# A small projection in the scan stage with two products a tile instead of three, its low-part rows added by VectorE, and C's rows copied apart

## What is computed

```python
xz = x @ W_in.T
x_proj, z = jnp.split(xz, 2, axis=-1)          # 1024 channels each
x_conv = _silu(conv_b + sum(xp[:, k:k + l, :] * conv_w[:, k] for k in range(4)))
x_dbl = x_conv @ W_xproj.T                      # 1024 channels to 33 values
Bmat, Cmat = x_dbl[..., :16], x_dbl[..., 16:32]
dt = jnp.clip(jax.nn.softplus(x_dbl[..., -1]), 0.001, 0.1)
# scan over time: h = exp(dt A) h + dt B x ;  y = h C
y = y * _silu(z) + x_conv * D_param
return y @ W_out.T
```

## Time and profile before

| | |
|---|---|
| runs, median (lowest to highest) | 2617.36 us (2613.93 to 2620.7) |
| the profiled execution: time | 2616.86 us |
| its span, first to last instruction | 2615.2 us |
| TensorE busy with products | 2416.5 us (92%), 16951 of them |
| TensorE loading weights | 2128.4 us (81%) |
| VectorE busy | 1492.4 us (57%) |
| ScalarE busy | 1199.3 us (46%) |
| GpSimd busy | 648.2 us (25%) |
| mean granted clock of TensorE, share of full | 0.969 |

### The profile page before, as it was taken

One profiled execution on the slowest core, in us unless ns is written; L12 is line 12 of the kernel. 1 busy time (PEld: TensorE's weight loads), 2 busy tenths in 40 slices (PEclk: granted clock), 3 DMA queues, 4 the chain that ended last, 5 costly groups with the idle time before them and its releaser, 6 DMA issues. The chain is left out here.

```text
span 2615.2 us, 47758 instructions
## 1 busy us (share of the span) xinstructions
PE 2416.5 (92%) x16951; PEld 2128.4 (81%) x16951; DVE 1492.4 (57%) x2583; ACT 1199.3 (46%) x1912; POOL 648.2 (25%) x1040
## 2 busy tenths in 40 slices
PE   5999999999997899999999983499999999999997
PEld 5899898998996688888888862288888888888886
DVE  5877877777774466666666655644334334333332
ACT  6655555655653444444444431044344444434342
POOL 3111111211214444444453521112030311203021
PEclk9999999999998999999999986699999999999999
DMA  4111111111115666666666532124241523424221
GB/s 122 48 37 42 47 38 39 47 38 47 40 39 160 168 182 175 180 181 178 179 162 186 154 102 84 52 89 112 93 108 65 140 74 105 119 80 108 84 65 20
DMA packets 236833, 261.01 MB, mean 100 GB/s; under 512 B 70312, under 2 KB 160424, under 8 KB 236560
## 3 DMA queue, kind: packets, MB, share of 16 engines
q1 hardware_dynamic: 195600, 237.48, 31.1%
q0 software_dynamic: 40960, 20.41, 4.4%
HBM read 182.47 MB, written 68.80 MB: 96 GB/s over the span
## 5 line engine op out<-in xcount | busy, mean ns | idle before, releaser
L420 PE MATMUL a_psP<-s_xnT_h,s_w_l 128*128 128x256 f32 x1024 | 298.5, 292 | 27.2 <-DVE s_xnT_l L667 17.0
L2243 DVE TENSOR_TENSOR d_h_l<-d_hf,d_h_h 128x616 fp32r<-128x616 f32 x124 | 99.2, 800 | 392.3 <-ACT d_h_h L2067 392.3
L1972 PE MATMUL d_psH<-d_xgT_h,d_w_l 128*128 128x308 f32 x1024 | 314.5, 307 | 3.0 <-ACT d_hf L2103 2.0
L1973 PE MATMUL d_psH<-d_xgT_l,d_w_h 128*128 128x308 f32 x1024 | 311.5, 304 | 0.0
L1974 PE MATMUL d_psH<-d_xgT_h,d_w_h 128*128 128x308 f32 x1024 | 311.3, 304 | 0.0
L2103 ACT ACTIVATE d_hf<-d_psH,d_b1c 128x308 f32<-128x308 f32 x256 | 130.7, 518 | 383.5 <-PE d_psH L1974 382.6
L421 PE MATMUL a_psP<-s_xnT_l,s_w_h 128*128 128x256 f32 x1024 | 290.9, 284 | 0.0
L422 PE MATMUL a_psP<-s_xnT_h,s_w_h 128*128 128x256 f32 x1024 | 290.5, 284 | 0.0
L1939 POOL DMA_INDIRECT out_dram<-d_ob,d_to x40 | 103.7, 2593 | 686.0 <-ACT d_ob L2120 675.9
L1972 PE MATMUL d_psO<-d_w_h,d_h_l 128*123 128x512 f32 x620 | 244.2, 394 | 0.0
L1973 PE MATMUL d_psO<-d_w_l,d_h_h 128*123 128x512 f32 x620 | 244.0, 394 | 0.0
(11 more groups left out here) (378 smaller groups left out, 6062.7 us busy)
## 6 DMA issues: line engine op xcount, KB each, us to landing
d_w<-in_W_dram SPq DMA_DIRECT2D x64, 1024.0 KB, 6.1
b_qst<-qs_d SPq DMA_DIRECT2D x48, 512.0 KB, 6.6
b_kst<-ks_d SPq DMA_DIRECT2D x48, 512.0 KB, 6.6
s_raw<-in_x_dram SPq DMA_DIRECT2D x16, 512.0 KB, 3.5
s_xres<-in_x_dram SPq DMA_DIRECT2D x16, 512.0 KB, 3.6
x_d<-s_xres SPq DMA_DIRECT2D x16, 512.0 KB, 2.8
s_raw<-in_ctxT_dram SPq DMA_DIRECT2D x16, 512.0 KB, 9.5
s_xres<-x_d SPq DMA_DIRECT2D x16, 512.0 KB, 9.3
```

What stands on the lines that cost most here:

```text
L420: pe.matmul(out, lo_w, hi_x, start=first, stop=False)
L1972: pe.matmul(out, lo_w, hi_x, start=first, stop=False)
L1973: pe.matmul(out, hi_w, lo_x, start=False, stop=False)
L2243: dve.tensor_tensor(out, a, b_, ALU.subtract).then_inc(done, 1)
```

## The change

`x_dbl` has 33 output columns, of which the 128 x 128 weight tile used 48 (dt is repeated 16 times). The change puts the weights' low parts into columns of their own of the same tile: the high parts of B and C in columns 0 to 31, their low parts in 32 to 63, dt's high part in 64 to 79 and its low part in 96 to 111. A second tile, `wx_l`, now holds the high parts alone. So `x_dbl(i)` has two passes: the wide tile by the high data, and the high weights by the low data. In `psX` the low parts' sums lie on partitions 32 to 63 and 96 to 111, and `rows_1` has five instructions instead of three: it copies both groups of low rows, adds dt, limits it, and adds B and C at once. C's rows now lie on partitions 16 to 31 of `rows`, below B's, and have copies of their own into `every`: eight of 256 columns as soon as `rows_1` is done, and eight of 513 columns for B and lam as before. The semaphores' counts follow.

```diff
-        rows, every = sb("rows", [N, 3 * S + 1]), sb("every", [P, 3 * S + 1])
-        Bb, Cr, lam = rows[:, 0:S], rows[:, S:2 * S], rows[:, 2 * S:]
+        rows, every = sb("rows", [2 * N, 2 * S + 1]), sb("every", [P, 3 * S + 1])
+        Bb, Cr, lam = rows[0:N, 0:S], rows[N:2 * N, 0:S], rows[0:N, S:]
...
                     wait(sp, rows_c, 2 * b)
                     sp.sem_inc(passed_s, 1)
+                    sp.wait_ge(rows_a, 5 * b + 5)
+                    for i in range(NB):
+                        sp.dma_start(every[i * N:(i + 1) * N, 2 * S + 1:], Cr).then_inc(every_ld, 16)
                     sp.wait_ge(rows_b, 12 * b + 5)
                     for i in range(NB):
-                        sp.dma_start(every[i * N:(i + 1) * N, :], rows[:]).then_inc(every_ld, 16)
+                        sp.dma_start(every[i * N:(i + 1) * N, 0:2 * S + 1], rows[0:N, :]).then_inc(every_ld, 16)
...
-                    split_mm(psX[:, 0:S], wx_h[:, i, :], wx_l[:, i, :], xcr_h[:, i % 3, :], xcr_l[:, i % 3, :],
-                             i == 0, i == KE - 1).then_inc(xd_mm, 1)
+
+                    pe.matmul(psX[:, 0:S], wx_h[:, i, :], xcr_h[:, i % 3, :], start=i == 0, stop=False)
+                    pe.matmul(psX[:, 0:S], wx_l[:, i, :], xcr_l[:, i % 3, :], start=False, stop=i == KE - 1).then_inc(xd_mm, 1)
...
-                        act.wait_ge(rows_a, 3 * b + 3)
+                        act.wait_ge(rows_a, 5 * b + 4)
...
-                cols = [(wx_raw[:, :, 0:N], slice(0, N)), (wx_raw[:, :, N:2 * N], slice(32, 32 + N)),
-                        (wx_raw[:, :, 2 * N:2 * N + 1].broadcast_to([P, KE, N]), slice(64, 64 + N))]
-                for src, at in cols:
-                    ins = dve.tensor_copy(wx_h[:, :, at], src)
+
+                cols = [(wx_raw[:, :, 0:2 * N], 0, 2 * N),
+                        (wx_raw[:, :, 2 * N:2 * N + 1].broadcast_to([P, KE, N]), 64, N)]
+                for src, at, n in cols:
+                    dve.tensor_copy(wx_l[:, :, at:at + n], src)
+                    ins = dve.tensor_copy(wx_h[:, :, at:at + n], src)
                 ins.then_inc(setup_dve, 1)
                 dve.wait_ge(setup_dve, 2)
-                for src, at in cols:
-                    ins = dve.tensor_tensor(wx_l[:, :, at], src, f32(wx_h[:, :, at]), ALU.subtract)
+                for src, at, n in cols:
+                    ins = dve.tensor_tensor(wx_h[:, :, at + 32:at + 32 + n], src, f32(wx_h[:, :, at:at + n]), ALU.subtract)
...
-                    wait(dve, every_ld, 16 * NB * b)
+                    wait(dve, every_ld, 32 * NB * b)
                     wait(dve, m_mm, b)
-                    dve.tensor_scalar(dt_r[:], psX[64:64 + N, 0:S], 5.0, None, ALU.min).then_inc(rows_a, 1)
-                    dve.tensor_copy(Bb, psX[0:N, 0:S]).then_inc(rows_a, 1)
-                    dve.tensor_copy(Cr, psX[32:32 + N, 0:S]).then_inc(rows_a, 1)
+
+                    dve.tensor_copy(dt_r[:], psX[96:96 + N, 0:S]).then_inc(rows_a, 1)
+                    dve.tensor_copy(rows[:, 0:S], psX[32:64, 0:S]).then_inc(rows_a, 1)
+                    dve.wait_ge(rows_a, 5 * b + 2)
+                    dve.tensor_tensor(dt_r[:], psX[64:64 + N, 0:S], dt_r[:], ALU.add).then_inc(rows_a, 1)
+                    dve.wait_ge(rows_a, 5 * b + 3)
+                    dve.tensor_scalar(dt_r[:], dt_r[:], 5.0, None, ALU.min).then_inc(rows_a, 1)
+                    dve.tensor_tensor(rows[:, 0:S], psX[0:32, 0:S], rows[:, 0:S], ALU.add).then_inc(rows_a, 1)
...
-                        dve.wait_ge(every_ld, 16 * NB * b + 16 * NB)
+                        dve.wait_ge(every_ld, 32 * NB * b + 32 * NB)
```

More of the change, by code:

```diff
@@ L689, in _ @@
             dve.memset(ones_row[:], 1.0).then_inc(setup_dve, 1)
-            dve.memset(rows[:, 2 * S:2 * S + 1], 0.0).then_inc(setup_act, 1)
+            dve.memset(rows[0:N, S:S + 1], 0.0).then_inc(setup_act, 1)
             dve.memset(fl[:], 0.0).then_inc(setup_act, 1)
@@ L781, in rows_2 @@
                         dve.wait_ge(exps_a, 2 * b + 2)
-                        dve.wait_ge(rows_a, 3 * b + 3)
+                        dve.wait_ge(rows_a, 5 * b + 5)
                         ch.did(dve.tensor_scalar(dt_r[:], dt_r[:], 0.001, 0.1, ALU.max, ALU.min))
@@ L799, in rows_2 @@
                         ch.n = 7
-                        dve.wait_ge(every_ld, 16 * NB * b + 16 * NB)
+                        dve.wait_ge(every_ld, 32 * NB * b + 32 * NB)
                         if first:
                             dve.wait_ge(setup_pool, 11)
-                        sums = every[:, 2 * S:]
+                        sums, C_ = every[:, S:2 * S + 1], every[:, 2 * S + 1:]
                         ch.did(dve.tensor_tensor(refm[:], sums[:, 0:S].rearrange("p (i t) -> p i t", t=BL)[:, :, 0], mine[:, :, 0], ALU.mult))
-                        ch.did(dve.tensor_tensor(every[:, S:2 * S], every[:, S:2 * S], mine[:].rearrange("p i t -> p (i t)"), ALU.mult))
+                        ch.did(dve.tensor_tensor(C_, C_, mine[:].rearrange("p i t -> p (i t)"), ALU.mult))
                         ch.wait()
@@ L814, in rows_3 @@
                     dve.tensor_tensor(EB[:], EB[:], every[:, 0:S], ALU.mult).then_inc(rows_c, 1)
-                    dve.tensor_tensor(EC[:], EC[:], every[:, S:2 * S], ALU.mult).then_inc(rows_c, 1)
+                    dve.tensor_tensor(EC[:], EC[:], every[:, 2 * S + 1:], ALU.mult).then_inc(rows_c, 1)
                 def bounds(part):
```

## The result

| | before | after |
|---|---|---|
| runs, median (lowest to highest) | 2617.25 us (2613.93 to 2620.7) | 2638.03 us (2636.28 to 2641.72) |
| ratio to before, 95% interval | | 1.0084 (1.0069 to 1.0098) |
| the profiled execution: time, span | 2616.86, 2615.2 us | 2636.66, 2635.0 us |

What follows compares the result with a forecast made beforehand. It took TensorE, 97% busy in the scan stage, as the bound, with waits at x_dbl and Y(3). 15 x 0.45 = 6.8 us gained less 1.8 us in batch 0 gave 5.0 us less, 2612.4 us, range 2605 to 2619 us.

Steps and rivals of the forecast that it cites:

- The loop's gain, 0.45 us: Scan stage: eight products less per batch, partly lost waiting for z(1), gain 0.45 us per batch, 6.8 us over 15.
- The chain: Scan batch, x_dbl(5) to Y(3): earlier x_dbl tiles bring dt's Exp, z(1)'s taking out and Y(3) forward, 0.54 us at Y(3).
- `rows_1`: VectorE in the scan stage: five instructions, 0.45 us per copy or addition and 0.28 for the limit; dt complete at 1.63 us.
- Batch 0: Scan stage's first batch: SyncE's sixteen copies have no cover, VectorE waits at `every`; 1.8 us charged once, between 0 and 3.
- Copies in the loop: SyncE in the scan loop: C's eight additional copies are covered by VectorE's `rows_2`, with 1 us to spare; no charge.
- The first rival: Scan stage: only TensorE's work counts, all 0.96 us arrives per batch, 12.6 us less, 2604.8 us; chance 0.14.
- The third rival: Scan stage: the longer `rows_1` holds Y(3) back, 0.23 us more per batch, 2622.7 us, or 12.3 us more; chance 0.10.
- The second rival: Scan stage: saved time goes into x_dbl's own waits, gain 0 to 0.1 us per batch, 2618.4 us; chance 0.13.
- the prediction's 5.0 us: Whole kernel: 6.8 us gained in the scan loop less 1.8 us lost in batch 0, so 5.0 us less.

Runs made afterwards that it cites:

- e2: The kernel before, nothing of the change, with 160 more TensorE instructions (80 idle transposes): 2641.12 us, ratio to before 1.0095.
- e5: The kernel after with 256 more TensorE instructions (128 idle transposes), one whole 16 KB packet: 2637.3 us, ratio to before 1.0076.
- e4: The kernel of e1 with C's eight copies of batch 0 issued early, in SyncE's list of weights: 2609.12 us.
- e10: The kernel of e1 without VectorE's additions of the low rows, the weights' low parts left out of the results: 2609.51 us, ratio to before 0.997.
- e9: The kernel before without the x_dbl pass of the low weights, with 48 idle transposes in batch 0: 2612.28 us, ratio to before 0.9987.
- e3: The kernel after with a third product in every x_dbl tile (low parts of x issued twice): 2618.78 us, ratio to before 1.0018.
- e1: The kernel after with 96 more TensorE instructions (48 idle transposes) in batch 0 of the scan stage: 2609.41 us, ratio to before 0.9979.
- e7: The kernel after with 144 more TensorE instructions (idle transposes): 2613.5 us, ratio to before 0.9987.
- e11: The kernel of e4 with 120 more TensorE instructions instead of 96: 2610.13 us, ratio to before 0.9971.
- e6: The kernel after with 48 more TensorE instructions (24 idle transposes in batch 0): 2621.2 us, ratio to before 1.0017.

## Why the prediction was wrong

**The step that failed** is one that the prediction took without a word: that the stages which the change doesn't touch take the time they took. Its sum had entries for the engines' work and SyncE's copies in the scan stage, and put attention and the length of the program at nothing without a reason. The list ahead of attention has 96 instructions less, and that moved all later packets of TensorE's program. In attention this cost 22.1 us. The 2.3 us ahead of the first logits came and went with it: that stretch takes 143.6 to 144.5 us in the three slow kernels (after, e2, e5) and 140.8 to 142.4 in the ten others. In the terms that it had the prediction was 1.8 us off (5.9 - 2.7 = 3.2 us gained for 5.0), and in the end 25.6.

- *The loop's gain, 0.45 us.* It was 0.38 (48.19 to 47.81). The chain held step by step in the batch shown: x_dbl(5) did not move; x_dbl(6) gained 0.40 (taken 0.45), x_dbl(7) 0.51 (0.57), Y(3) 0.46 (0.54), the period 0.37 (0.46 before rounding). Most of what was missing came in at x_dbl(6). Over 15 periods it is 5.9 us for 6.8.
- *`rows_1`.* 0.45 us a step for the two copies and the addition of dt, one of the copies on 32 partitions, and 0.28 for the limit, as priced.
- *Batch 0.* VectorE waited 2.12 us at `every` for the 1.8 taken, and the stretch from x_dbl(7) to the scan matrix grew by 2.06; e4 took that away. The other 0.7 us were not in the sum.
- *Copies in the loop.* Covered, as forecast: C's eight are issued from 331.90 to 336.88 us in the batch shown, the other eight from 338.03 on, and e10 against e9 shows no cost. The Trainium skill's rule on small transfers ("DMA: Bandwidth & Descriptors", Rules for kernel authors) holds for batch 0 alone.
- *The first rival*, all of 0.96 us, is refuted by e9: without VectorE's additions 0.50 arrives. The Trainium skill's rule on the busiest engine ("Perfetto Trace Analysis", Identifying the Most-Contended Engine) names TensorE rightly, but about half of the work taken off it comes back as waits.
- *The third rival* was priced at 0.23 us a batch for a `rows_1` that begins where it did. In e3, where TensorE's part is undone, the period is longer by just that, 0.23; in the kernel after it does not apply.
- *The second rival*, that x_dbl(6) and (7) come no earlier, did not happen: they came 0.40 and 0.51 us earlier.

With the packets put back (e1) the kernel gave 2609.4 us beside a before of 2616.1, 6.7 us less; the prediction's 5.0 us are inside that interval (2.4 to 8.6 us). That nearness is in part luck. e1's span is 8.7 us shorter than that of before, and only 4.5 of it lie in the scan stage (6.3 gained in the 15 periods, 1.7 lost in batch 0); attention gave 1.6 us and the stretch behind it 2.3, where the prediction had nothing.

**Open.** The trace does not name the DMA engine of a packet. That it is the same engine which is late is read from the rate of a sixteenth, and from the 8 or 16 packets that start as the program's packet ends. The third packet stands at 37.9 to 38.1 us in e1, e7 and e11, though the program moved by up to 48 instructions; in e6 it wanders from batch to batch. What holds it there was not tried. The path by which the 2 us ahead of the first logits are lost was not followed. Nor was it tried to make the stores of k less easily disturbed.

## What to carry to other kernels

When a change alters the number of instructions in a written-out list, the packets of all the program behind it can fall among other transfers. If a stage far away gets slower or faster, look at the program's queue in the transfer view first, and put the length back with idle instructions before the change is judged; two or three lengths tell how much of a difference is this. In this kernel the stage that felt it is the one whose next loads wait for the landing of a small store.

## What the runs showed of the hardware

- TensorE's program comes in packets of 16 KB on a queue of its own, 108 in 2.6 ms. Such a packet takes 0.9 to 1.8 us on one DMA engine (median 1.1 in the attention of the kernel after) where the stores' packets of 1 KB take 0.05, and a store that shares the engine lands 0.5 to 2.1 us later.
- Up to 28.6 us of 2617, 1.1%, hang on where they fall (2609.4 us in e1 and 2638.0 in the kernel after, with the same work but for 48 idle transposes), and 256 instructions more give the old places again (e5, 2637.3 us).
- Out of PSUM a copy on 32 partitions takes VectorE no longer than one on 16, and an addition no longer than a copy: the next instruction starts 0.45 us later for 256 columns (`rows_1` of the kernel after).
